# Moving the cast of the normalised rows from ScalarE to VectorE in a post-norm transformer layer

## Chip, cores and metric

One Trainium2 chip, all 8 cores, each working on one sequence of the batch with no exchange between them. The metric is the device time in microseconds of the slowest core. Five engines of a core appear below: TensorE (PE; its weight loads are PEld), VectorE (DVE), ScalarE (ACT), GpSimd (POOL) and SyncE (SP).

## What is computed

One layer on x of shape (8, 4096, 1024), f32: attention inside blocks of 64 tokens with 16 heads of 64, output projection, residual and LayerNorm; then a gated feed-forward part with hidden size 3072, residual and LayerNorm.

```python
qkv = x @ W_qkv.T + b_qkv
attn = softmax(q*scaling @ k.T) within each block of 64 tokens
x = layernorm(x + (attn @ v) @ W_out.T + b_out)
h = silu(x @ (w_gate/127).T) * (x @ (w_up/127).T)
x = layernorm(x + h @ (w_down/127).T)
```

## The kernel before

A core works on its 4096 tokens in 16 tiles of 256, each tile in two blocks `st` of 128 tokens. `tile_front(t)` does V, attention, output projection and the first LayerNorm for one tile; `front_a(t)` does what comes ahead of it: cast of x to bf16 (L355), eight transposes per block through TensorE (L364), their copy out of PSUM (L371), and the 128 QK products of 256 columns (L389), which ScalarE evacuates (L397). Two tiles make a pair `s`, and `ffn(s)` does the feed-forward part for both: gate and up (L783), down (L838), second LayerNorm. The order, written out by hand, is for each pair: `tile_front(2s)`, `front_a(2s+1)`, `tile_front(2s+1)`, `front_a(2s+2)`, `ffn(s)`. In the first pair a stage is added that transposes the feed-forward weights by DMA (SyncE's queue, L289; stores by GpSimd's).

Every engine runs its own instructions strictly in this order; between engines there are semaphores. `P.do(engine, ...)` records one instruction; `inc` names the semaphore that it raises, `waits` what it waits for. A wait on the own engine's semaphore is left out unless it has a `!`. `P.acq` and `P.rel` hand over PSUM buffers: `ps23` is held by one user at a time.

The place of the change is the end of `tile_front`. The output projection of block 1 (L579, L585) ends; VectorE adds the residual (L591) and sums (L640), ScalarE squares (L651), small steps give mean and variance (L658 to L677), and VectorE normalises both blocks, L684, in place in `x1` (f32). Then for each block: a copy of its 1024 columns to bf16 in `aoT` (L698), eight transposes through TensorE into `ps23` (L706), and a copy out of PSUM into `x1T` by VectorE (L714), which releases `ps23` for the next block. In VectorE's order `front_a` of the next tile follows; after the last tile `ffn` does. `emit_qkv_chunk` in the setup has a cast of the same form on VectorE (L225).

Of the kernel before, what the change touches and what calls it, by code (L numbers as in the profile page):

```python
# [11 lines left out]
AF = mybir.ActivationFunctionType  # L12
# [87 lines left out]
def build_nc(n_tiles=NT, dbg=False):  # L100
# [5 lines left out]
    wout = nc.dram_tensor("wout", [E, E], F32, kind="ExternalInput").ap()  # L106
# [33 lines left out]
    with ExitStack() as ctx:  # L140
# [13 lines left out]
        aoT = en(nc.sbuf_tensor("aoT", [128, 2048], BF16))  # L154
# [29 lines left out]
        def body(P: Prog):  # L184
            mil = {}

            def xsrc(t):
                return x_in[t * TTOK:(t + 1) * TTOK, :].rearrange("(st pp) j -> pp st j", pp=128)
# [5 lines left out]
            for t in range(min(2, n_tiles)):  # L194
                P.do("gpsimd", lambda s, t=t: s.dma_start(
                    out=xf[:, (t % 2) * 2048:(t % 2) * 2048 + 2048].rearrange("p (st j) -> p st j", st=2),
                    in_=xsrc(t)), inc="sx" + str(t % 2), amt=16)
                mil["xload", t] = P.c["sx" + str(t % 2)]
            P.do("scalar", lambda s: s.activation(out=brow[0:1, 0:E], in_=stgb[0:1, :], func=AF.Copy),
                 inc="sc", waits=[("sp1", mil["consts"])])  # L200
            mil["bcast1"] = P.c["sc"]
            P.do("gpsimd", lambda s: s.dma_start(out=stgb[:], in_=bv_in), inc="sp4", amt=16,
                 waits=[("sc", mil["bcast1"])])
            mil["bvload"] = P.c["sp4"]
            P.do("scalar", lambda s: s.activation(out=brow[0:1, E:2 * E], in_=stgb[0:1, :], func=AF.Copy),
                 inc="sc", waits=[("sp4", mil["bvload"])])
            mil["bcast"] = P.c["sc"]
            P.do("vector", lambda v: v.tensor_scalar_mul(bqkvT[:, 0:KCH], bqkvT[:, 0:KCH], QSCALE),
                 inc="ve", waits=[("sp1", mil["consts"])])
# [3 lines left out]
            for cc in range(2):  # L213
                P.do("gpsimd", lambda g, cc=cc: g.dma_start(
                    out=wout_nat[:, cc * 512:(cc + 1) * 512],
                    in_=wout[:, cc * 512:(cc + 1) * 512]), inc="sgo" + str(cc), amt=16)
# [45 lines left out]
            for k in range(KCH):  # L262
                P.do("sync", lambda s, k=k: s.dma_start(  # L263
                    out=RWout[:, k * E:(k + 1) * E],
                    in_=wout_nat[:, k * 128:(k + 1) * 128], transpose=True),
                    inc="sp3", amt=16, waits=[("sgo" + str(k // 4), 16)])
# [143 lines left out]
            def tile_front(t):  # L410
# [8 lines left out]
                for st in range(2):  # L419
                    w = P.acq("ps23") + [("sc", mil["bcast"]), ("ve", mil["xt_evac", t, 1])]  # L420
                    for half in range(2):
                        for k in range(KCH):
# [5 lines left out]
                                waits=w if (half == 0 and k == 0) else ())  # L428
# [4 lines left out]
                            inc="pe" if half == 1 else None)  # L433
                    mil["v_mm", t, st] = P.c["pe"]
                    P.do("vector", lambda v, st=st: v.tensor_copy(  # L435
                        out=vtok[:, st * 1024:(st + 1) * 1024], in_=ps23[:]),
                        inc="ve", waits=[("pe", mil["v_mm", t, st]),
                                         ("sb2", mil.get("dump_vtok", 0))])
# [3 lines left out]
                if dbg and t == DBG_T:  # L442
                    P.do("gpsimd", lambda q: q.dma_start(out=dbg_t["d_xT"], in_=xT[:]),
                         inc="sb0", amt=16, waits=[("ve", mil["xt_evac", DBG_T, 1])])
                    mil["dump_xT"] = 16
                    P.do("gpsimd", lambda q: q.dma_start(out=dbg_t["d_qkT"], in_=qkT[:]),
                         inc="sb1", amt=16, waits=[("sc", mil["qk_done", DBG_T])])
                    mil["dump_qkT"] = 16
                    P.do("gpsimd", lambda q: q.dma_start(out=dbg_t["d_vtok"], in_=vtok[:]),
                         inc="sb2", amt=16, waits=[("ve", mil["v_evac", DBG_T, 1])])  # L450
# [166 lines left out]
                if t + 2 < n_tiles:  # L617
                    P.do("gpsimd", lambda s, t=t: s.dma_start(
                        out=xf[:, (t % 2) * 2048:(t % 2) * 2048 + 2048].rearrange("p (st j) -> p st j", st=2),
                        in_=xsrc(t + 2)), inc="sx" + str(t % 2), amt=16,  # L620
                        waits=[("ve", mil["resid1", t, 1])])
# [7 lines left out]
                if dbg and t == DBG_T:  # L629
                    P.do("gpsimd", lambda q: q.dma_start(out=dbg_t["d_aoT"], in_=aoT[:]),  # L630
                         inc="sb5", amt=16, waits=[("ve", mil["aoT", DBG_T, 1, 1])])
                    mil["dump_aoT"] = 16
                    P.do("gpsimd", lambda q: q.dma_start(out=dbg_t["d_x1a"], in_=x1[:, (DBG_T % 2) * 2048:(DBG_T % 2) * 2048 + 2048]),
                         inc="sb6", amt=16, waits=[("ve", mil["resid1", DBG_T, 1])])
                    mil["dump_x1a"] = 16

                if STAGE <= 7:
# [6 lines left out]
                    inc="ve", waits=[("ve!", mil["resid1", t, 1])])  # L644
                mil["lnsum", t] = P.c["ve"]
                for st in range(2):
                    pssq = ps45 if st == 0 else ps67
                    psname = "ps45" if st == 0 else "ps67"
                    xsl = x1[:, x1off + st * 1024: x1off + (st + 1) * 1024]
                    w = P.acq(psname)  # L650
                    P.do("scalar", lambda sC, xsl=xsl, pssq=pssq, st=st: sC.activation(  # L651
                        out=pssq[:], in_=xsl, func=AF.Square,
                        accum_out=stats[:, Q1 + st:Q1 + st + 1]),
                        inc="sc",
                        waits=w + [("ve", mil["resid1", t, st])])
# [4 lines left out]
                    inc="ve", waits=[("ve!", mil["lnsum", t])])  # L660
# [4 lines left out]
                    inc="ve", waits=[("ve!", mil["mean1", t])])  # L665
# [4 lines left out]
                    inc="ve", waits=[("sc", mil["square", t, 1]), ("ve!", mil["msq1", t])])  # L670
                mil["var1", t] = P.c["ve"]
                P.do("scalar", lambda sC: sC.activation(
                    out=stats[:, R1:R1 + 2], in_=stats[:, V1:V1 + 2], func=AF.Ln,
                    bias=stats[:, EPSC:EPSC + 1]),
                    inc="sc", waits=[("ve", mil["var1", t])])
                mil["lnln1", t] = P.c["sc"]
                P.do("scalar", lambda sC: sC.activation(  # L677
                    out=stats[:, R1:R1 + 2], in_=stats[:, R1:R1 + 2],
                    func=AF.Exp, scale=-0.5),
                    inc="sc", waits=[("sc!", mil["lnln1", t])])  # L680
                mil["rstd1", t] = P.c["sc"]
                for st in range(2):
                    xsl = x1[:, x1off + st * 1024: x1off + (st + 1) * 1024]
# [3 lines left out]
                        inc="ve", waits=([("sc", mil["rstd1", t]),  # L687
                                          ("sb6", mil.get("dump_x1a", 0))] if st == 0 else ()))
                    mil["norm1", t, st] = P.c["ve"]

                if dbg and t == DBG_T:
                    P.do("gpsimd", lambda q: q.dma_start(out=dbg_t["d_x1"], in_=x1[:, (DBG_T % 2) * 2048:(DBG_T % 2) * 2048 + 2048]),
                         inc="sb7", amt=16, waits=[("ve", mil["norm1", DBG_T, 1])])
                    mil["dump_x1"] = P.c["sb7"]

                for st in range(2):
                    xsl = x1[:, x1off + st * 1024: x1off + (st + 1) * 1024]
                    P.do("scalar", lambda sC, xsl=xsl, st=st: sC.activation(  # L698
                        out=aoT[:, st * 1024:(st + 1) * 1024], in_=xsl, func=AF.Copy),
                        inc="sc",  # L700
                        waits=[("ve", mil["norm1", t, st]), ("pe", mil["wout", t, 1]),
                               ("sb5", mil.get("dump_aoT", 0))])
                    mil["x1b", t, st] = P.c["sc"]
                    w = P.acq("ps23")
                    for c in range(KCH):
                        P.do("tensor", lambda tn, st=st, c=c: tn.matmul(  # L706
                            ps23[:, c * 128:(c + 1) * 128],
                            aoT[:, st * 1024 + c * 128: st * 1024 + (c + 1) * 128],
                            ident[:], start=True, stop=True),
                            inc="pe" if c == KCH - 1 else None,  # L710
                            waits=(w + [("sc", mil["x1b", t, st])]) if c == 0 else ())
                    mil["x1t_mm", t, st] = P.c["pe"]
                    l = p * 2 + st
                    P.do("vector", lambda v, l=l: v.tensor_copy(  # L714
                        out=x1T[:].rearrange("p (k j) -> p k j", j=512)[:, :, l * 128:l * 128 + 128],
                        in_=ps23[:].rearrange("p (k j) -> p k j", j=128)),
                        inc="ve",
                        waits=[("pe", mil["x1t_mm", t, st]),
                               ("pe", mil.get(("gu_done", s - 1), 0) if (t % 2 == 0 and st == 0) else 0)])
                    mil["x1t_evac", t, st] = P.c["ve"]  # L720
                    P.rel("ps23", "ve")
# [207 lines left out]
            for s in range(n_tiles // 2):  # L929
                tile_front(2 * s)  # L930
                if STAGE <= 8:
                    break
                if not EARLY_A:
                    front_a(2 * s + 1)
                if s == 0:
                    emit_prep_casts2()
                tile_front(2 * s + 1)
                if not EARLY_A and 2 * s + 2 < n_tiles:
                    front_a(2 * s + 2)
                ffn(s)  # L940
                if STAGE <= 10:
                    break
# [76 lines left out]
```

How the kernel before makes its waits and increments, by code:

```python
    def do(self, engname, emit=None, inc=None, amt=1, waits=()):  # L67
        if engname == self.live:
            eng = self.eng[engname]
            for (s, v) in waits:
                force = s.endswith("!")
                if force:
                    s = s[:-1]
                if v <= 0 or (SEM_PROD[s] == engname and not force):
                    continue
                if v <= self._waited[s]:
                    continue
                eng.wait_ge(self.sems[s], v)
                self._waited[s] = v
            inst = emit(eng)
            if inc is not None:
                inst.then_inc(self.sems[inc], amt)
        if inc is not None:
            self.c[inc] += amt
# [99 lines left out]
        def body(P: Prog):  # L184
# [751 lines left out]
                    emit_prep_casts2()  # L936
                tile_front(2 * s + 1)
                if not EARLY_A and 2 * s + 2 < n_tiles:
                    front_a(2 * s + 2)
                ffn(s)
                if STAGE <= 10:
                    break
            for nm in SEM_PROD:
                if P.c[nm] > 0 and SEM_PROD[nm] != "sync":
                    P.do("sync", lambda sq, nm=nm, v=P.c[nm]: sq.wait_ge(sems[nm], v))
            for nm in SEM_PROD:
                if P.c[nm] > 0 and SEM_PROD[nm] == "sync":
                    P.do("sync", lambda sq, nm=nm, v=P.c[nm]: sq.wait_ge(sems[nm], v))
```

## Time and profile before

| | us |
|---|---|
| runs of the kernel | 2730.4, 2891.5 (median 2811.0) |
| profiled execution, its own time | 2741.3 |
| its span on the slowest core | 2739.8 |
| TensorE products busy | 2022.0 (74% of the span) |
| VectorE busy | 799.3 (29%) |
| ScalarE busy | 469.0 (17%) |

The span runs from the first to the last instruction of the slowest core. Busy time tells how much an engine did, not whether something waited for it; that is in the chain of work that ended last, and in the idle time before an instruction together with what ended it. "PEclk" is the clock that TensorE was granted, as a share of 2.4 GHz.

### The profile page before, as it was taken

To read this page: it belongs to the slowest core of one execution; us is meant where nothing else is said; L and a number is where in the kernel's file an instruction comes from. 1 tells how busy PE (TensorE), PEld (TensorE's weight loads), DVE (VectorE), ACT (ScalarE), POOL (GpSimd) and SP (SyncE) were. 2 spreads that over 40 slices of the span, in tenths; PEclk is the share of its full clock that TensorE was granted. 3 is DMA by queue.
4 is the path that set the end of the run, shared out by engine and by line. 5 is a ranking of instruction groups with operands and counts; after the bars stand their busy time and mean duration, and the time that the engine had idled before them with its cause. 6 is when DMAs were issued, how large, how long until landed. Compare 5 with 4: busy or idle time off the path is not lost.

```text
span 2739.8 us, 27267 instructions; the slowest of 8 cores (2720.8 to 2739.8 us)
## 1 busy us (share of the span) xinstructions
PE 2022.0 (74%) x10560; PEld 999.3 (36%) x10560; DVE 799.3 (29%) x1282; ACT 469.0 (17%) x867; POOL 66.9 (2%) x111
## 2 busy tenths in 40 slices
PE   1567229776797679976797678976698588976795
PEld 1333214224443335434443344434443244433342
DVE  2443001043321441143322432143311532133411
ACT  0112101012210122012211122112211122112210
POOL 1100000100000000000000000000000000000000
PEclk9967669867898679977799678977799678987798
DMA  9999994620143002510053102510043102520033
GB/s 168 164 113 124 222 230 148 134 97 31 39 142 128 16 32 79 159 54 31 16 154 108 47 30 71 159 64 31 16 139 123 46 16 77 154 77 16 23 116 108
DMA packets 258830, 253.55 MB, mean 93 GB/s; under 512 B 88608, under 2 KB 221744, under 8 KB 258128
## 3 DMA queue, kind: packets, MB, share of 16 engines
q1 hardware_dynamic: 216576, 121.65, 17.7%
q0 software_dynamic: 19280, 86.11, 14.2%
q10 hardware_dynamic: 22848, 44.05, 4.9%
q8 instruction: 87, 1.43, 0.2%
q14 instruction: 39, 0.32, 0.0%
HBM read 216.13 MB, written 56.62 MB: 100 GB/s over the span
## 4 chain that ended last, share of the span: by engine, by line
PE 57%; DVE 15%; SPq 9%; DMA 9%; issue 3%; another core or an unknown queue 3%; ACT 3%; DVEq 0%; POOL 0%; ACTq 0%; POOLq 0%
PE ps L783 24%; PE ps L389 8%; PE ps L838 8%; SPq L289 7%; PE ps L579 6%; DMA wdb<-wdT_s 4%; PE ps L423 3%; DMA wdb<-wd_nat 2%; DVE diag L508 2%; DVE stats L491 2%; PE ps L472 2%; PE ps L466 2%; SPq L263 2%; DVE x L861 1%
## 5 line engine op out<-in xcount | busy, mean ns | idle before, releaser
L783 PE MATMUL ps<-x1T,wgu 128*128 128x512 bf16 x3072 | 670.9, 381 | 98.6 <-DMA wgu<-wuT_s 97.1
L783 PEld LDWEIGHTS ps<-x1T,wgu 128*128 128x128 bf16 x3072 | 301.9, 98 | 465.0 <-issue 108.4
L838 PE MATMUL ps<-wdb,hT 128*128 128x512 bf16 x1536 | 351.3, 385 | 51.9 <-DMA wdb<-wdT_s 23.3
L801 DVE TENSOR_TENSOR hT<-silu,ps 128x512 bf16<-128x512 bf16 x192 | 132.0, 688 | 751.1 <-PE ps L783 519.9
L389 PE MATMUL ps<-xT,RWqkv 128*128 128x256 bf16 x2048 | 260.5, 295 | 23.6 <-DVE xT L371 23.6
L838 PEld LDWEIGHTS ps<-wdb,hT 128*128 128x128 bf16 x1536 | 146.8, 99 | 256.4 <-issue 97.8
L389 PEld LDWEIGHTS ps<-xT,RWqkv 128*128 128x128 bf16 x2048 | 201.6, 105 | 82.3 <-issue 27.4
L423 PE MATMUL ps<-RWqkv,xT 128*128 128x512 bf16 x512 | 146.0, 437 | 87.0 <-DVE vtok L435 60.0
L579 PE MATMUL ps<-RWout,aoT 128*128 128x512 bf16 x512 | 179.1, 513 | 35.1 <-DVE aoT L567 35.1
L795 ACT ACTIVATE silu<-ps 128x512 bf16<-128x512 f32 x192 | 114.6, 597 | 523.5 <-PE ps L783 523.4
L397 ACT ACTIVATE qkT<-ps,bqkvT_s 128x256 bf16<-128x256 f32 x256 | 121.4, 474 | 401.1 <-PE ps L389 401.1
L861 DVE SCALAR_TENSOR_TENSOR x<-ps,x 128x1024 f32<-128x1024 f32 x32 | 37.0, 1218 | 397.6 <-PE ps L838 397.6
L706 PE MATMUL ps<-ident_s,aoT 128*128 128x128 bf16 x256 | 32.3, 305 | 145.6 <-ACT aoT L698 120.0
L466 PE MATMUL ps<-qkT 64*128 64x128 bf16 x512 | 136.1, 266 | 0.0
L472 PE MATMUL ps<-augcS 4*128 4x128 bf16 x512 | 136.0, 266 | 0.0
L479 ACT ACTIVATE expb<-ps 128x1024 bf16<-128x1024 f32 x64 | 65.5, 1024 | 339.8 <-PE ps L472 339.8
L435 DVE CAST vtok<-ps 128x1024 bf16<-128x1024 f32 x32 | 39.2, 1224 | 282.0 <-PE ps L429 282.0
L423 PEld LDWEIGHTS ps<-RWqkv,xT 128*128 128x128 bf16 x512 | 50.8, 107 | 164.2 <-issue 129.8
L491 DVE TENSOR_REDUCE stats<-expb 128x8 f32<-128x1024 bf16 x64 | 78.0, 1220 | 98.7 <-ACT expb L479 95.8
L870 ACT ACTIVATE ps<-x 128x1024 f32<-128x1024 f32 x32 | 32.9, 1028 | 422.4 <-DVE x L861 422.4
L579 PEld LDWEIGHTS ps<-RWout,aoT 128*128 128x128 bf16 x512 | 56.8, 121 | 131.2 <-issue 112.1
L508 DVE TENSOR_SCALAR diag<-ident_s,stats 128x128 bf16<-128x128 bf16 x512 | 89.3, 251 | 45.3 <-ACT stats L501 45.3
(71 smaller groups left out, 1080.2 us busy)
## 6 DMA issues: line engine op xcount, KB each, us to landing
wgu<-wgT_s SPq DMA_DIRECT2D x64, 768.0 KB, 4.9
wgu<-wuT_s SPq DMA_DIRECT2D x64, 768.0 KB, 6.9
wdb<-wdT_s ACTq DMA_DIRECT2D x84, 512.0 KB, 3.6
xf<-x POOLq DMA_DIRECT2D x16, 1024.0 KB, 5.2
y<-x POOLq DMA_DIRECT2D x16, 1024.0 KB, 5.6
x<-wqkv POOLq DMA_DIRECT2D x24, 512.0 KB, 10.9
wg_nat<-wg POOLq DMA_DIRECT2D x1, 6144.0 KB, 64.1
wu_nat<-wu POOLq DMA_DIRECT2D x1, 6144.0 KB, 122.4
```

The lines of the kernel that those rows point to most:

```text
L289: P.do("sync", lambda q, nat=nat, k=k, stg=stg: q.dma_start(out=stg, in_=nat[:, k * 128:(k + 1) * 128], transpose=True), inc="spt" + str(p ...
L389: P.do("tensor", lambda tn, c=c, k=k, bank=bank: tn.matmul(ps01[:, bank * 512:bank * 512 + 256], RWqkv[:, k * 3 * E + c * 128: k * 3 * E + ...
L397: P.do("scalar", lambda sC, c=c, bank=bank: sC.activation(out=qkT[:, c * 256:(c + 1) * 256], in_=ps01[:, bank * 512:bank * 512 + 256], fun ...
L423: P.do("tensor", lambda tn, st=st, half=half, k=k: tn.matmul(ps23[:, half * 512:(half + 1) * 512], xT[:, k * 256 + st * 128: k * 256 + st ...
L466: P.do("tensor", lambda tn, st=st, slot=slot, qpo=qpo, qc=qc, kc=kc, pst=pst: tn.matmul(pst[:, slot * 128:(slot + 1) * 128], qkT[qpo:qpo + ...
L472: P.do("tensor", lambda tn, slot=slot, qpo=qpo, pst=pst: tn.matmul(pst[:, slot * 128:(slot + 1) * 128], augcS[qpo:qpo + 4, 0:128], augcS[q ...
L491: P.do("vector", lambda v, col=col, eo=eo: v.reduce_sum(stats[:, SUMS + col * 8:SUMS + col * 8 + 8].rearrange("p (g o) -> p g o", g=8), ex ...
L508: P.do("vector", lambda v, h8=h8, hh=hh, eo=eo: v.tensor_scalar_mul(diag[:, eo + h8 * 128:eo + (h8 + 1) * 128], ident[:], stats[:, RCPC + ...
L579: P.do("tensor", lambda tn, st=st, half=half, k=k: tn.matmul(ps23[:, half * 512:(half + 1) * 512], aoT[:, k * 256 + st * 128: k * 256 + st ...
L783: P.do("tensor", lambda tn, wi=wi, k=k, mi_=mi_, boff=boff, pair=pair: tn.matmul(pair[:, wi * 512:(wi + 1) * 512], wgu[:, boff + wi * (KCH ...
L801: P.do("vector", lambda v, m=m, pair=pair: v.tensor_tensor(hT[:, m * 512:(m + 1) * 512], silu2[:, (m % 2) * 512:(m % 2 + 1) * 512], pair[: ...
L838: P.do("tensor", lambda tn, m=m, l=l, half=half, wslot=wslot, coff=coff: tn.matmul(psl[l][:, half * 512:(half + 1) * 512], hT[:, m * 512 + ...
```

## The change

The two f32 to bf16 copies of each tile at L698 are issued to VectorE as `tensor_copy` instead of to ScalarE as an activation with `Copy`. Their semaphore is VectorE's, TensorE waits for that one, and each copy waits explicitly for the normalisation of its block, which is on the same engine. In VectorE's order a tile now reads: both L684, copy of block 0, L714 of block 0, copy of block 1, L714 of block 1. Nothing else is changed: 32 instructions in all.

```diff
-                    P.do("scalar", lambda sC, xsl=xsl, st=st: sC.activation(
-                        out=aoT[:, st * 1024:(st + 1) * 1024], in_=xsl, func=AF.Copy),
-                        inc="sc",
-                        waits=[("ve", mil["norm1", t, st]), ("pe", mil["wout", t, 1]),
+                    P.do("vector", lambda v, xsl=xsl, st=st: v.tensor_copy(
+                        out=aoT[:, st * 1024:(st + 1) * 1024], in_=xsl),
+                        inc="ve",
+                        waits=[("ve!", mil["norm1", t, st]), ("pe", mil["wout", t, 1]),
                                ("sb5", mil.get("dump_aoT", 0))])
-                    mil["x1b", t, st] = P.c["sc"]
+                    mil["x1b", t, st] = P.c["ve"]
                     w = P.acq("ps23")
                     for c in range(KCH):
                         P.do("tensor", lambda tn, st=st, c=c: tn.matmul(
@@
-                            waits=(w + [("sc", mil["x1b", t, st])]) if c == 0 else ())
+                            waits=(w + [("ve", mil["x1b", t, st])]) if c == 0 else ())
```

## Rows read from the trace of the kernel before

**Rows 1.** Spans and mean granted TensorE clock of the cores.

```profile
core 5: 2739.8 us, clock 0.828
...
core 7: 2720.8 us, clock 0.832
```

**Rows 2.** The chain that ended last, by engine, from the page.

```profile
PE 57%; DVE 15%; SPq 9%; DMA 9%; issue 3%; another core or an unknown queue 3%; ACT 3%; DVEq 0%; POOL 0%; ACTq 0%; POOLq 0%
```

**Rows 3.** Groups by line: busy us, mean ns; idle before, what ended it.

```profile
L783 PE MATMUL ps<-x1T,wgu 128*128 128x512 bf16 x3072 | 670.9, 381 | 98.6 <-DMA wgu<-wuT_s 97.1 <-DVE x1T L714 1.5
L838 PE MATMUL ps<-wdb,hT 128*128 128x512 bf16 x1536 | 351.3, 385 | 51.9 <-DMA wdb<-wdT_s 23.3 <-DMA wdb<-wd_nat 20.0 <-DVE hT L801 7.5
...
L397 ACT ACTIVATE qkT<-ps,bqkvT_s 128x256 bf16<-128x256 f32 x256 | 121.4, 474 | 401.1 <-PE ps L389 401.1
...
L706 PE MATMUL ps<-ident_s,aoT 128*128 128x128 bf16 x256 | 32.3, 305 | 145.6 <-ACT aoT L698 120.0 <-DVE x1T L714 25.6
...
L698 ACT ACTIVATE aoT<-x 128x1024 bf16<-128x1024 f32 x32 | 32.0, 1049 | 17.1 <-DVE x L684 17.1
...
L684 DVE TENSOR_SCALAR x<-x,stats 128x1024 f32<-128x1024 f32 x32 | 24.6, 810 | 12.7 <-ACT stats L677 12.7
```

**Rows 4.** Timeline of tile 7's end: start, us, instructions, idle before.

```profile
1332.24 1.53 DVE L684 TENSOR_SCALAR x<-x,stats 128x1024 f32<-128x1024 f32 x2 [0.79 <-ACT stats L677]
1333.20 2.00 ACT L698 ACTIVATE aoT<-x 128x1024 bf16<-128x1024 f32 x2 [1.07 <-DVE x L684]
...
1334.40 1.01 PE L706 MATMUL ps<-ident_s,aoT 128*128 128x128 bf16 x8 [7.48 <-ACT aoT L698]
1335.52 1.23 DVE L714 CAST x1T<-ps 128x1024 bf16<-128x1024 f32 x1 [1.75 <-PE ps L706]
...
1336.99 1.01 PE L706 MATMUL ps<-ident_s,aoT 128*128 128x128 bf16 x8 [1.58 <-DVE x1T L714]
1338.11 1.23 DVE L714 CAST x1T<-ps 128x1024 bf16<-128x1024 f32 x1 [1.37 <-PE ps L706]
1339.25 1.22 DVE L355 CAST xb<-xf 128x2048 bf16<-128x2048 f32 x1
...
1340.62 1.01 PE L364 MATMUL ps<-ident_s,xb 128*128 128x128 bf16 x8 [2.61 <-DVE xb L355]
```

**Rows 5.** Line L225: duration in ns min/median/max, first and last start.

```profile
L225 DVE CAST hT<-x x24: 682/693/741, 41.7 to 105.9; 128x1024 bf16<-128x1024 f32 x24
```

**Rows 6.** The chain in order of time, first stage: start, us, what.

```profile
163.49 116.10 SPq L289
```

**Rows 7.** Timeline of ScalarE, tiles 1 and 0.

```profile
271.71 2.00 ACT L698 ACTIVATE aoT<-x 128x1024 bf16<-128x1024 f32 x2 [1.07 <-DVE x L684]
...
187.03 2.00 ACT L698 ACTIVATE aoT<-x 128x1024 bf16<-128x1024 f32 x2 [1.07 <-DVE x L684]
```

**Rows 8.** The chain, QK stretches of tiles 6 and 7, and of tile 8.

```profile
1260.62 17.02 PE ps L389 x128
...
1345.59 15.54 PE ps L389 x128
...
1571.42 16.93 PE ps L389 x128
```

**Rows 9.** Stretches of 1 us: busy time of engines, PEclk, DMA share, GB/s.

```profile
1266.00:1267.00 1.00, 1.00 (x9) 0.76 (x8) 0.00 (x0) 0.46 (x1) 0.00 (x0) 0.73 0.00 0
...
1348.00:1349.00 1.00, 1.00 (x9) 0.79 (x8) 0.00 (x0) 0.05 (x2) 0.00 (x0) 0.77 0.00 0
```

**Rows 10.** The chain, gate and up products of pairs 6 and 7.

```profile
2292.98 82.89 PE ps L783 x384
...
2581.99 85.76 PE ps L783 x384
```

**Rows 11.** The chain, first V products of tiles 6 and 8 on it.

```profile
1195.84 3.57 PE ps L423 x8
...
1508.26 3.57 PE ps L423 x8
```

## The prediction

> **What bounds the kernel now.** First the cores: the spans lie between 2720.8 (core 7) and 2739.8 us (core 5), at a mean clock near 0.83, so core 5 stands for the chip [rows 1]. Then the chain that ended last, by line: TensorE's products carry 57% of it and VectorE 15%; ScalarE has only 3% [rows 2]. So the engine that loses work here (ScalarE) is not a bound, and the one that gains it (VectorE) sits on the chain. What matters is the place of the moved copy, and for that the groups by line: all 16 first copies of a tile are waited for by TensorE, 120.0 us of idle time for L706 (7.5 each, the whole LayerNorm among them), and a further 25.6 us go to the wait for the VectorE copy out of PSUM at L714 [rows 3]. In every tile the transposes of x1 are thus a relay in which TensorE has nothing else to do.
>
> **The relay before, in one tile.** The timeline of tile 7 shows it [rows 4]. Normalisations (L684) start at 1332.24 and run 1.53 us for two; ScalarE's copies start at 1333.20 (2.00 for two); transposes at 1334.40; L714 at 1335.52; second transposes at 1336.99; second L714 at 1338.11; the next tile's cast L355 at 1339.25; its transposes at 1340.62. From first normalisation to first transposes: 2.16 us. From the first L714 to the second transposes: 1.47, which is L714 alone, because the second ScalarE copy ended at 1335.20, long before.
>
> **The change, part by part.** It takes 32 copies off ScalarE (1.05 us each [rows 3]) and gives VectorE 32 copies from an f32 tile in SBUF to a bf16 tile in SBUF, 128x1024. The trace has exactly this form on VectorE at L225: 0.682 to 0.741 us, median 0.693 [rows 5]. Bounds: below, half of the 128x2048 cast L355, 0.61; above, the same size out of PSUM, L714, 1.23 [rows 4]. I take 0.69. It is 0.36 shorter than ScalarE's, but order counts more, as VectorE works its program in order: both normalisations, copy 0, L714 of block 0 (which waits for TensorE), copy 1, L714 of block 1.
>
> First transposes: the second normalisation now stands before copy 0. A normalisation takes 0.81 [rows 3] and the two 1.53, so they start 0.72 apart and copy 0 starts 1.44 to 1.53 after the first; then 0.69, and 0.15 from VectorE's end to TensorE's start (L355 at 1339.25 plus 1.22, transposes at 1340.62 [rows 4]). That is 2.28 to 2.37 against 2.16: 0.12 to 0.21 later. I take 0.12, since satisfied waits still let VectorE's instructions follow closely (L355 started 0.09 before L714 had ended [rows 4]).
>
> Second transposes: copy 1 now stands behind the first L714. It starts 1.14 after L714 does (as L355 behind the second L714, 1339.25 - 1338.11), then 0.69 + 0.15: 1.98 against 1.47, 0.51 later. This copy lay free beside the transposes and now lies on the path. What follows (second L714, L355, its transposes) keeps its distances. Sum: 0.12 + 0.51 = 0.63 us later per tile.
>
> The new waits are on VectorE's own normalisations, which have ended when they are reached: nothing. TensorE's wait changes its semaphore, not its number: nothing. Behind the removed copies on ScalarE stands only the evacuation of the next QK products, for which it sat idle 401.1 us [rows 3], so an earlier free ScalarE brings nothing. Behind the added copies on VectorE stand L714, L355 and, for odd tiles, the first product of the feed-forward part (it waited 1.5 us for L714 in the last pair [rows 3]). No DMA is moved; the load of x on GpSimd waits for L591, ahead of all this.
>
> How often it counts: tiles 0 and 1 (ScalarE's copies at 187 and 272 us) lie inside the first stage, where the chain is in the weight transposes on the SyncE queue, from 163.49 us for 116.10 in one piece, to 279.6 [rows 6, 7]. Their 0.63 is hidden by that. Tiles 2 to 15 count: 14 x 0.63 = 8.8 us if nothing else moved.
>
> **The clock.** What follows the relay is a stretch of 128 QK products (L389), begun at the low level (0.50, 1.2 GHz) and finished at the full one (1.00, 2.4 GHz). After an even tile it took 16.9 to 17.0 us in all seven cases, after an odd one 15.5 in all six [rows 8]. The difference is the moment at which the clock rises: tile 6's stretch starts at 1260.62 and the clock rises at about 1266.54, 5.9 us on (0.73 in that microsecond); tile 7's starts at 1345.59 and it rises at about 1348.46, 2.9 us on [rows 9]. Setting 5.9 low + 11.1 full and 2.9 low + 12.6 full both equal to 128 products gives 4.7 and 9.0 products per us: a low microsecond does 0.52 of a full one. So if a start comes d later and the rise stays, the end is only 0.52 d later.
>
> Even tile: the start is 0.63 later, the rise 5.3 us on; I take the rise as unmoved, the end is 0.33 later. Odd tile: its start is 0.33 + 0.63 = 0.96 later. With an unmoved rise only 1.9 us of work would stand before it; the rows show 2.9 and 5.9 and nothing shorter. I take it that the rise then comes later, near what even tiles have, and the stretch takes about 16.8 instead of 15.5 (17.0 is the upper end, 15.1 the lower, with the rise unmoved). So 0.96 + 1.3 = 2.26 us per pair for the six pairs from tiles 2 and 3 to 12 and 13: 13.6. The last pair has no QK stretch behind it; its feed-forward part begins low (85.76 against 82.89 us for the same 384 products [rows 10]) and with its rise unmoved gives half of 0.96: 0.5. Sum 14.1 us.
>
> A rule speaks to this: the Trainium skill, "TensorE: Matmul & The Clock Gate", section "Part 1: The HAM clock gate", says that the gate's observation is free-running and that a clock change depends on where the first matmul lands in it. By that rule too a late start can meet the rise late or unmoved; the two kinds of stretch in rows 8 and 9 agree, and the sum above comes from those rows.
>
> After that a pair's delay passes the feed-forward part (VectorE and transfers started by TensorE itself, so they move along) and enters the V products and attention of the next even tile. From V product to QK start this took 64.8 us (1195.84 to 1260.62) in one pair and 63.2 (1508.26 to 1571.42) in another [rows 8, 11], again by where the clock rises. I take 0 on average, with bounds of about 6 us either way (seven pairs, up to 0.8 each).
>
> **The sum.** The profiled execution is 2741.3 us long by its own time (span 2739.8). 2741.3 + 14.1 = 2755. The two runs shown are 2730.4 and 2891.5 with a median of 2811.0; my sum is against the profiled execution and lies near the lower run.
>
> **Rivals.**
> - *The rise stays put after odd tiles too.* The stretch shortens to 15.1 and a pair is 0.96 x 0.52 = 0.5 late: 7 x 0.5 = 3.5, time 2745. For it: the clock does not know of the kernel. Against: no rise under 2.9 us on. 0.15.
> - *Hidden altogether* (the transfers of the down stage, L838, had been late for other reasons and absorb it): 2741. For it: TensorE waited 23.3 us for wdb [rows 3]. Against: those transfers start on TensorE's progress. 0.08.
> - *Faster by the clock in the attention stretch.* With the rise unmoved (3.5) and all seven V-to-QK stretches at their short end (-6): -2.5, time 2739. 0.07.
> - *Faster by the shorter copy.* If the engine's duration alone counted, 14 x 0.36 = 5.0 us would be gained: 2736. For it: 1.05 against 0.69 [rows 3, 5]; against: the order worked out above. The Trainium skill, "Perfetto Trace Analysis", section "Optimizing Scalar/DVE Operations", says an operation that either engine can do is faster on VectorE where a performance mode exists; the durations agree, the order is what it leaves out. 0.05.
> - *The copy runs at the speed of L714*, 1.23: 2 x 0.54 x 14 = 15.1 more, time 2770. For it: all other 1024-wide casts on this path. Against: L225. 0.08.
> - *Slower by over 2%*: the clock stays low for whole QK stretches. 128 products at 4.7 per us are 27.2 us, 10.2 and 11.7 over today's, 22 per pair; from the third pair on it exceeds 55 us, e.g. 2741 + 66 = 2807. Against: it rose in all thirteen. 0.02.
>
> **How the numbers follow.** My forecast has 0.55. The range must hold also the rivals from 2736 to 2770 and the lower run as a base (2730 + 3.5): 2732 to 2775. That leaves out the last rival and the tails of the others, less than 0.2. About 2% (55 us) is what a measurement of this kernel can tell from no change; only the last rival and an error of fourfold reach it: slower 0.03, faster 0.01, same 0.96.
>
> **What would show it.** VectorE copies near 0.69 us with TensorE's second transposes 1.98 after the first L714 began; from first normalisation to the QK start 0.63 longer (13.35 to 13.98); even stretches 16.7, odd ones 16.8. Odd stretches at 15.1 speak for the first rival; copies of 1.2 for the fifth. If VectorE waited before copy 0, or if the spans of both kernels were equal with these distances changed, my account of what lies on the path would be wrong.

## The result and the profile after

| | before | after |
|---|---|---|
| median of all runs, us | 2742.0 (15 runs) | 2813.7 (16 runs) |
| lowest, us | 2729.3 | 2749.2 |
| profiled execution, us | 2741.3 | 2750.3 |
| its spans, eight cores, us | 2720.8 to 2739.8 | 2729.1 to 2748.7 |
| mean of these spans, us | 2728.8 | 2741.5 |

The medians hold runs in which the cores of one die (in one run of both) ran at a lower granted clock, about 0.74 to 0.81, and took up to 200 us longer, 9 of the 16 runs after and 5 of the 15 before, and every ratio below compares only runs without that. By these the changed kernel takes 1.0058 times the time of the kernel before, 95% interval 1.0037 to 1.0079: 16 us more. That is within the 2% called "same" here, but it is a loss.

The timeline of the changed kernel's slowest core, end of tile 7 (start, us, engine, line, instructions, idle time before and what ended it):

```profile
1331.54 1.53 DVE L684 TENSOR_SCALAR x<-x,stats 128x1024 f32<-128x1024 f32 x2 [0.79 <-ACT stats L677]
1332.98 0.69 DVE L698 CAST aoT<-x 128x1024 bf16<-128x1024 f32 x1
...
1333.82 1.01 PE L706 MATMUL ps<-ident_s,aoT 128*128 128x128 bf16 x8 [7.60 <-DVE aoT L698]
1334.94 1.23 DVE L714 CAST x1T<-ps 128x1024 bf16<-128x1024 f32 x1 [1.27 <-PE ps L706]
1336.08 0.69 DVE L698 CAST aoT<-x 128x1024 bf16<-128x1024 f32 x1
...
1336.91 1.01 PE L706 MATMUL ps<-ident_s,aoT 128*128 128x128 bf16 x8 [2.08 <-DVE aoT L698]
1338.03 1.23 DVE L714 CAST x1T<-ps 128x1024 bf16<-128x1024 f32 x1 [1.27 <-PE ps L706]
1339.17 1.22 DVE L355 CAST xb<-xf 128x2048 bf16<-128x2048 f32 x1
```

Beside [rows 4]: first transposes 2.28 us after the first normalisation (before 2.16), second transposes 1.97 after the first L714 (before 1.47). The copy itself takes 0.69 instead of 1.05, and VectorE never sits idle ahead of it (0.0 in its row below); but copy 1 starts only at 1336.08, 1.14 after L714 started. The groups by line say the same in one row: TensorE's idle time ahead of L706 grew from 145.6 to 155.2 us and all of it now ends on the copy (in [rows 3] 25.6 us ended on L714):

```profile
L706 PE MATMUL ps<-ident_s,aoT 128*128 128x128 bf16 x256 | 32.4, 307 | 155.2 <-DVE aoT L698 155.2
...
L698 DVE CAST aoT<-x 128x1024 bf16<-128x1024 f32 x32 | 21.9, 686 | 0.0
```

The QK stretches in the chain of work in order of time (start, us, what), an even tile and the odd one after it, and the microsecond in which the clock rises in the odd one (columns as in [rows 9]):

```profile
1260.21 16.70 PE ps L389 x128
...
1345.51 16.72 PE ps L389 x128
```

```profile
1349.00:1350.00 1.00, 1.00 (x7) 0.67 (x6) 0.00 (x0) 0.47 (x1) 0.00 (x0) 0.50 0.00 0
1350.00:1351.00 1.00, 1.00 (x7) 0.72 (x6) 0.00 (x0) 0.12 (x1) 0.00 (x0) 0.60 0.00 0
```

In [rows 8] the odd stretch took 15.54. Now the clock rises at 1350.8, 5.3 us after the stretch began, where before it was 2.9, so the odd tile pays 1.2 us more, and the even one 0.3 less because its start comes later while its rise stays.

One slowest core is a thin base, so the following table takes all eight cores of each profiled execution: from the timelines, the time in pieces of the program, added up per core and averaged. "Front" is everything from the end of one down stage to the QK start, from the QK end to the next QK start, and in the last pair to the first feed-forward product: 14 relays, all exposed. "QK" is the 7 even and 6 odd stretches. "Transfer-bound" is the first stage and the down stages, which differ by several us between executions of whatever kernel. The last columns are the mean odd stretch and how many of 48 odd stretches had their clock rise under 4.4 us after their start. Stretches are counted here to the start of their last product, 0.11 us less than in rows that give their length. What the table leaves out, mostly the gate and up products, is 616 to 617 us in each of the three executions.

| us, mean of 8 cores | front | QK | transfer-bound | odd stretch | early rises |
|---|---|---|---|---|---|
| before | 1030.1 | 210.7 | 871.8 | 15.61 | 41 |
| before, a second execution | 1030.6 | 211.0 | 870.2 | 15.65 | 40 |
| after | 1039.5 | 215.2 | 870.7 | 16.59 | 0 |

Front +9.4 and QK +4.5: 13.9 us. These two are the change; the two executions of the kernel before differ in them by 0.5 and 0.3. They are sums over parts of the program, and stand beside the 12.7 us by which the mean span grew and the 16 us (10 to 22) of the ratio.

### The profile page after: what moved, and what is told of

The parts are those of the page before. It is cut to its first block, busy times and chain, and to the rows that moved or that the text cites. A ratio compares the mean times of both kernels' runs of the same rounds, so it can differ in the third digit from the quotient of the medians.

```text
span 2748.7 us, 27253 instructions; the slowest of 8 cores (2729.1 to 2748.7 us)
## 1 busy us (share of the span) xinstructions
PE 2021.3 (74%) x10560; PEld 1002.4 (36%) x10560; DVE 817.8 (30%) x1314; ACT 436.5 (16%) x835; POOL 67.1 (2%) x111
## 3 DMA queue, kind: packets, MB, share of 16 engines
q0 software_dynamic: 19280, 86.11, 14.1%
## 4 chain that ended last, share of the span: by engine, by line
PE 56%; DVE 15%; DMA 9%; SPq 9%; issue 4%; another core or an unknown queue 3%; ACT 2%; DVEq 0%; POOL 0%; ACTq 0%; POOLq 0%
PE ps L783 24%; PE ps L389 8%; SPq L289 8%; PE ps L838 7%; PE ps L579 6%; DMA wdb<-wdT_s 5%; PE ps L423 3%; DMA wdb<-wd_nat 2%; PE ps L472 2%; PE ps L466 2%; DVE diag L508 2%; DVE stats L491 2%; DVE x L861 1%; DVE stats L880 1%
## 5 line engine op out<-in xcount | busy, mean ns | idle before, releaser
L389 PE MATMUL ps<-xT,RWqkv 128*128 128x256 bf16 x2048 | 267.9, 300 | 23.9 <-DVE xT L371 23.6
L389 PEld LDWEIGHTS ps<-xT,RWqkv 128*128 128x128 bf16 x2048 | 205.7, 107 | 85.8 <-issue 28.2
L423 PE MATMUL ps<-RWqkv,xT 128*128 128x512 bf16 x512 | 144.7, 434 | 87.1 <-DVE vtok L435 60.1
L706 PE MATMUL ps<-ident_s,aoT 128*128 128x128 bf16 x256 | 32.4, 307 | 155.2 <-DVE aoT L698 155.2
L423 PEld LDWEIGHTS ps<-RWqkv,xT 128*128 128x128 bf16 x512 | 50.6, 107 | 163.2 <-issue 128.3
```

Source lines behind the costliest of these rows:

```text
L389: P.do("tensor", lambda tn, c=c, k=k, bank=bank: tn.matmul(ps01[:, bank * 512:bank * 512 + 256], RWqkv[:, k * 3 * E + c * 128: k * 3 * E + ...
L423: P.do("tensor", lambda tn, st=st, half=half, k=k: tn.matmul(ps23[:, half * 512:(half + 1) * 512], xT[:, k * 256 + st * 128: k * 256 + st ...
```

## Experiments

Each ratio is to the kernel before, measured beside it on the same chip; front and QK are against the first row of the table. The theory: the order in VectorE's queue lengthens the relay by 0.63 us per tile, and the later start of odd QK stretches costs them the early clock rise.

**Only block 0's copy moved.**

```diff
-  P.do("scalar", ... out=aoT[block st], in_=x1[block st])
+  P.do("vector" if st == 0 else "scalar", ...)
```

> Only block 0's copy is on VectorE, block 1's stays on ScalarE. My theory (place in VectorE's order): first transposes 2.28 us after the first normalisation instead of 2.16, second transposes still 1.47 after the first L714, first normalisation to QK start 13.47 (before 13.35, after 13.97); the QK stretch after odd tiles keeps its early clock rise and stays at 15.4 to 15.5 us; the whole +1 to +2 us over before. Rival A (the copy's own duration counts, 0.69 for 1.05): 5 us faster than before. Rival B (any copy on VectorE costs alike): half of the change's loss, +8.

Measured: 2742.1 and 2743.6 us, too few comparable runs for an interval, so only the trace speaks. First normalisation (1323.99) to QK start (1337.47) 13.48 us, as expected. Front +3.6 over before (expected 1.7), QK +2.5. But only 19 of 48 odd stretches kept the early rise; I had expected all. Core 0 has both kinds, an odd stretch at 709.58 and one at 1644.95:

```profile
709.58 15.45 PE ps L389 x128
...
1644.95 17.06 PE ps L389 x128
```

The early rises that are left came 2.63 to 2.73 us after the start (before: 2.64 to 2.87 in two executions), the others 5.4 to 6.0. The kernel before sat next to the edge: 0.12 us more is enough for many to fall over it. Front and QK together, 6.1 us, lie nearer to rival B's 8 than to my 1 to 2; what speaks against B is the relay, 0.13 us longer here and 0.49 in the next kernel.

**Only block 1's copy moved** (`st == 1` in the line above).

> Only block 1's copy is on VectorE. Theory: first transposes at 2.16, second transposes 1.98 after the first L714, first normalisation to QK start 13.86; stretch after odd tiles goes over to the late clock rise, about 16.8; the whole +11 to +14 us. Rival B (any copy on VectorE costs alike): +8. Rival A: faster.

Measured: 1.0043 (1.0017 to 1.0069), 12 us; normalisation to QK start 1328.06 to 1341.90, 13.84; no early rise left, odd stretches 16.66; front +7.7, QK +3.1. The copy that lay beside the transposes is the one that costs, four times what copy 0 adds to the relay.

**Both copies on VectorE, but ahead of L714.**

```diff
   for st in range(2):
       P.do("vector", ... tensor_copy(out=aoT[block st], in_=x1[block st]))
+  for st in range(2):
       transposes (L706); copy out of PSUM (L714)
```

> Both copies on VectorE as in the changed kernel, but both ahead of block 0's L714 in its order. Theory: copy 1 lies beside the first transposes, second transposes at 1.47 after L714, first normalisation to QK start 13.47; odd stretches 15.4 to 15.5; the whole +1 to +2 us over before. Rival (VectorE's added work or its memory traffic costs, not the order): the same +16 as the changed kernel.

The timeline of tile 7 (L707 and L715 are L706 and L714 there):

```profile
1323.88 1.53 DVE L684 TENSOR_SCALAR x<-x,stats 128x1024 f32<-128x1024 f32 x2 [0.79 <-ACT stats L677]
1325.33 1.29 DVE L698 CAST aoT<-x 128x1024 bf16<-128x1024 f32 x2
...
1326.16 1.01 PE L707 MATMUL ps<-ident_s,aoT 128*128 128x128 bf16 x8 [7.60 <-DVE aoT L698]
1327.28 1.22 DVE L715 CAST x1T<-ps 128x1024 bf16<-128x1024 f32 x1 [0.66 <-PE ps L707]
...
1329.77 1.23 DVE L715 CAST x1T<-ps 128x1024 bf16<-128x1024 f32 x1 [1.26 <-PE ps L707]
```

With the same 32 copies on VectorE the relay is back to 13.37 us (1323.88 to 1337.25, before 13.35): the front is +1.0 instead of +9.4. So the lengthening comes from the order, not from VectorE's added work. It is 0.1 shorter than I had put it, because the two L715 start 2.49 apart where the two L714 of [rows 4] start 2.59 apart. The trace shows why: from the first of them to the second transposes it is 1.37 us in all 128 tiles of the eight cores, before 1.48 in 116 of 128 (1.47 by the rounded times of [rows 4]). Ahead of the second transposes the kernel before has TensorE wait for VectorE's L714 and then for ScalarE's copy, which had ended long ago; with both copies ahead, `P.do` leaves the wait for the copy out, as an earlier wait on the same semaphore covers it. A wait that is already satisfied thus costs 0.1 us where it stands behind the one that ends last. Yet the whole is 1.0038 (1.0004 to 1.0072), 10 us, not the 1 to 2 us expected: 33 of 48 odd stretches rise late, QK is +5.6. That is the clock's part nearly alone. The interval overlaps the changed kernel's, so the whole time doesn't decide between theory and rival here; the front does. Whether the 0.02 us in the relay, or the 0.1 us between the end of an even QK stretch and the start of the odd one (68.07 against 67.97 on the mean), is what tips them was not separated.

**A delay and nothing else.** The kernel before with an idle cast ahead of L355:

```diff
+ P.do("vector", lambda v: v.tensor_copy(out=silu2[:, 0:1024], in_=xf[first 1024 columns]))
  P.do("vector", ... tensor_copy(out=xb[:], in_=xf[...]))      # L355
```

> The kernel before with both copies on ScalarE and an extra VectorE cast of 1024 columns, whose result nothing uses, ahead of every L355, so the QK start comes 0.6 us later without any other part of the change. Theory: even stretches 16.7, odd 16.8 (late rise), the whole +13 to +16 us, like the changed kernel. Rival (the clock's part is not from the delay but from the engines' order or the last pair): odd stretches stay 15.5 or shrink to 15.1 and the whole is +4 to +9 us.

Measured: 1.0045 (1.0028 to 1.0062), 12 us. First normalisation (1331.83) to QK start (1345.79) is 13.96 us, as in the changed kernel. No early rise left, odd stretches 16.60; front +7.3, QK +2.9. It is a little below the expected 13 to 16 and its interval overlaps the changed kernel's. The change's loss comes back, with both copies on ScalarE, from a late QK start alone.

**The delay doubled.** A second such cast (to `expb`).

> As the delay-only kernel, but with two idle casts: the QK starts come 1.2 us later than before instead of 0.6. Theory (the clock's part is a step already taken at the first 0.6 us, further delay only shifts within it): odd and even rises about 4.0 to 4.8 us after the start, stretches 16.2 to 16.4, no longer than in the delay-only kernel; whole +4 to +10 us over the delay-only kernel, i.e. 1.006 to 1.008 times before. Rival (each delay costs in proportion, step or not): twice the delay-only kernel's loss, 1.009.

Measured: 1.0064 (1.0047 to 1.0081), 18 us over before, 5 more than with one cast. Front +14.4, another 7.1; but QK is 1.0 us under the kernel before, 3.9 less than with one cast. The chain of core 5, an even and an odd stretch (L396 is L389 there):

```profile
1878.32 15.47 PE ps L396 x128
1961.96 16.30 PE ps L396 x128
```

Odd rises now come 4.0 to 4.7 us after the start, odd stretches 16.26. The clock's cost is a step, taken at the first tenths of a microsecond; more delay gives part of it back (an odd stretch is 0.65 us longer than before, where one cast made it 0.99). Doubling the delay doubled the front's loss and cancelled the stretches' loss.

**TensorE kept busy through the relay.** Products nobody uses, in idle time, from tile 2 on: 30 ahead of the first x1 transposes, 4 ahead of the second, 9 ahead of the first x transposes, 4 and 4 behind.

```diff
+ def fill(n, ps): n times matmul(ps[:, 0:512], RWqkv[:, 0:128], RWqkv[:, 0:512])
+ fill(30 if st == 0 else 4, ps01)     # ahead of L706, block st
+ fill(9, ps01); fill(4, ps67)         # ahead of L364, blocks 0 and 1
+ fill(4, ps67)                        # ahead of L389
```

> The kernel before, with products that nothing uses put into TensorE's idle time around the transposes of x1 and of the next x (30 ahead of the first x1 transposes, 4, 9, 4 and 4 in the gaps behind, from tile 2 on), so that the QK stretch starts at full clock. Theory (both stretches pay for a low start): QK stretches of 14.2 us after even and odd tiles alike, the fillers lie in idle time: about 7 x 2.7 + 6 x 1.3 = 27 us faster than before. Rival: the fillers themselves delay the relay, or the clock falls all the same, and nothing is gained.

Measured: 0.9841 (0.9828 to 0.9854), 44 us faster, where 27 were expected. Timeline of core 0, tile 7 (L720, L728, L374 and L401 are L706, L714, L364 and L389; L356 is the filler, of whose four products in the second row one has no record):

```profile
1306.21 0.61 PE L720 MATMUL ps<-ident_s,aoT 128*128 128x128 bf16 x8 [0.90 <-ACT aoT L710]
...
1306.87 0.81 PE L356 MATMUL ps<-RWqkv 128*128 128x512 bf16 x3
...
1311.62 0.61 PE L374 MATMUL ps<-ident_s,xb 128*128 128x128 bf16 x8 [0.67 <-DVE xb L361]
...
1315.79 14.15 PE L401 MATMUL ps<-xT,RWqkv 128*128 128x256 bf16 x128 [0.61 <-DVE xT L381]
```

All 104 stretches are at 14.0 to 14.2 us (QK -28.1). What I had left out are the four groups of transposes, 0.61 us instead of 1.01, each on the relay: 1304.05 to 1315.79 is 11.74 us, 1.61 less than before; front -21.0. The first stage, where there are no fillers, took 9.9 us longer in this execution. It did so in all five kernels with fillers of this document: 544.8 to 550.0 us on the mean of the cores, against 537.0 to 541.0 in the nine executions without. Nothing here tells why.

**The same fillers in the changed kernel.**

> The same fillers in the changed kernel. Theory: with the clock's part removed only the longer relay is left, 14 x 0.63 = 9 us over the filled kernel before, QK stretches 14.2. Rival (the change costs as much whatever the clock does): +15 over the filled kernel before.

Measured: 0.9841 (0.9828 to 0.9854), the same as without the change. In the timelines the relay is 12.35 us against 11.74 (1310.63 to 1322.98), and the front is 7.2 us and QK 0.6 longer, 7.8 in all, near the 8.5 that 14 times 0.61 makes. In the whole time this does not show, though the two intervals leave room for only some 5 us either way: the forecast of 9 was missed. In the profiled executions transfer-bound stages were 9.4 us shorter; by the mean span of the eight cores over the four comparable runs of each, the changed kernel is 3.3 us longer (2689.3 against 2686.0, and runs of one kernel differ by more than that). So the direct part is shown in the stages and not in the whole; whether transfers took it up or the runs are too few is open. What is gone is the step in the odd stretches, 14.04 and 14.05.

**No copy on the path.** VectorE writes the normalised block as bf16 at once, and the f32 normalisation in place comes after the next tile's L371.

```diff
- tensor_scalar(x1[st], x1[st], mean, rstd); tensor_copy(aoT[st], x1[st])
+ tensor_scalar(aoT[st], x1[st], mean, rstd)        # bf16, L684
+ tensor_scalar(x1[st], x1[st], mean, rstd)         # f32, after front_a, L695
```

> No copy on the path at all: VectorE writes the normalised block as bf16 into aoT directly (tensor_scalar), and the f32 normalisation in place follows after the next tile's x transposes, beside the QK products. Theory: first transposes 0.95 us after the start of the first normalisation instead of 2.16, relay 1.2 us shorter than before; the QK starts move to where even rises come under 4 us on, even stretches about 15.7, and the whole is 20 to 30 us faster than before. If the clock gave nothing back: 14 x 1.2 = 17 us faster. Rival (the relay is not what sets the end): no change.

Measured: 0.9917 (0.9902 to 0.9932), 23 us faster. Timeline of core 4 (L710 and L718 are L706 and L714):

```profile
1318.78 1.54 DVE L684 TENSOR_SCALAR aoT<-x,stats 128x1024 bf16<-128x1024 f32 x2 [0.79 <-ACT stats L677]
...
1319.74 1.01 PE L710 MATMUL ps<-ident_s,aoT 128*128 128x128 bf16 x8 [6.28 <-DVE aoT L684]
1320.86 1.23 DVE L718 CAST x1T<-ps 128x1024 bf16<-128x1024 f32 x1 [0.54 <-PE ps L710]
...
1322.23 1.01 PE L710 MATMUL ps<-ident_s,aoT 128*128 128x128 bf16 x8 [1.48 <-DVE x1T L718]
...
1330.60 1.53 DVE L695 TENSOR_SCALAR x<-x,stats 128x1024 f32<-128x1024 f32 x2
...
1330.83 15.94 PE L389 MATMUL ps<-xT,RWqkv 128*128 128x256 bf16 x128 [1.48 <-DVE xT L371]
```

The transposes start 0.96 us after the normalisation and the f32 one lies beside the QK products. The relay is 12.05 us, 1.3 shorter: the 1.2 expected, and the 0.1 of the wait that is left out here too. Front -20.0, QK -3.4: as expected even rises mostly moved under 4 us (45 of 56), odd ones to 3.3 to 3.9; even stretches are 16.05 on the mean, not the 15.7 expected.

**Both, with 30 and with 24 fillers.**

> Both: direct bf16 and fillers. Theory: QK stretches 14.2 and relay 1.2 shorter: about 17 us faster than the filled kernel before. Rival: the fillers ahead of the first transposes now reach into the path (30 of them take 6.5 us or more, and the idle time has shrunk to 6.3), so it is no faster than the direct version alone.

> The direct bf16 version with fillers, 24 instead of 30 ahead of the first transposes, so that they end before the transposes' input is there. Theory: 0.2 to 0.4 us per tile from tile 2 on, 3 to 5 us faster than the version with 30, i.e. 0.974 to 0.976 times before; QK stretches still 14.1. Rival (24 are too few to hold the clock): stretches back at 15.5 or more and slower than the version with 30.

Measured: 0.9763 (0.9748 to 0.9777) and 0.9747 (0.9727 to 0.9767); QK 183.2 in both. Direct bf16 takes another 21 us off the filled kernel, where 17 were expected. With 24 instead of 30 fillers the front is only 0.7 us shorter; the expected 3 to 5 us is not shown, the intervals overlap.

**Fillers in the V products too**, 28 between the two blocks of every even tile, where TensorE waits for the second LayerNorm.

> As the former, and 28 fillers more between the V products of the two blocks of every even tile from tile 2 on, where TensorE waits 6.8 us for the second LayerNorm on VectorE. Theory: the second block's first 8 V products take 1.9 instead of 3.6 us and the first scores run at full clock: 2 to 4 us per pair, 14 to 25 us in all, 0.966 to 0.970 times before. Rival (the clock falls again in the attention whatever came before it, and VectorE sets the pace there): at most the 1.7 us of the V products, of which nothing shows, 0.974.

Measured: 0.9704 (0.9685 to 0.9723), 81 us faster than before and the best version of this study. The first products after the wait, in the chain, changed kernel and this one (L437 is L423 there):

```profile
1507.01 3.57 PE ps L423 x8
```

```profile
1467.20 1.89 PE ps L437 x8
```

The way from the down stage to the QK start became 2.0 us shorter per pair (front -14.4 for all), 1.7 of it in this row. By the ratios this kernel is 12 us faster than the one without these fillers, by the front 14: at or just under the low end of what I expected. The attention behind it gained 0.3 us.

**The kernel before once more**, for the spread of the clock's rises.

> The kernel before itself, once more, to see how much the clock's rises vary from one execution to the next. Theory (they follow from the distances in the program): again about 40 of 48 odd stretches with the early rise, 15.6 us on the mean over all cores. Rival (they vary by execution, and the 7 late ones of the first trace were few by chance): 20 or more of 48 late, and then the late rises of the kernel with both copies ahead of L714 are no effect of its order.

Measured: 40 of 48 early, mean odd stretch 15.65 (first trace 41, 15.61). Core 7's odd stretches, four of its six:

```profile
684.54 15.51 PE ps L389 x128
...
998.53 15.52 PE ps L389 x128
...
1309.21 15.50 PE ps L389 x128
...
1934.11 17.03 PE ps L389 x128
```

The pattern belongs to the program's distances and not to one execution, so the 33 late ones with the copies ahead, of which there is one execution, are taken as an effect of that kernel.

## Why the prediction was right or wrong

- **The relay, 0.12 + 0.51.** Right to 0.01 us at each step: 2.28, 1.97 (1.98 forecast), normalisation to QK start 13.97 (13.98). VectorE's copy was 0.69. Copies ahead of L714 take the relay's loss away at equal work; the delay-only kernel brings it back without the move. One reading was off: the 1.47 us before were not "L714 alone" but 1.37, and 0.10 for the second wait; in the changed kernel that wait ends last, so the sum isn't touched.
- **14 exposed tiles, 8.8 us.** The front is +9.4. Tiles 0 and 1 are hidden: the first stage is 540.2 us before and 540.5 after.
- **The clock, even tiles.** Forecast 16.7 us; measured 16.61 to 16.96 on the slowest core, -1.4 us for all seven (all cores), forecast -2.1.
- **The clock, odd tiles.** Forecast 16.8; measured 16.59 to 16.77 on the slowest core. For the six, +5.8 us against the 7.8 of the sum (1.3 each): on the mean an odd stretch grew by 0.98, because 7 of 48 had been late already and the late rise comes at 5.0 to 5.4 and not at 5.9. The prediction's "15.5 in all six" was one core's.
- **The V products and attention, 0 on average.** Their part of the front is included in the +9.4, of which the relays make 8.7 (14 times 0.62); nothing of the feared 6 us either way is seen.
- **The sum.** +14.1 forecast, which is a ratio of 1.0050; measured 1.0058 (1.0037 to 1.0079), and +13.9 in front and QK of the traces. The class, within 2%, was right too. Rivals: the rise did not stay put (0 of 48), nothing was hidden, the attention stretch gave nothing, the shorter copy gained nothing, the copy ran at 0.69, and no stretch stayed low throughout.
- **What was wrong is the base of the predicted time and with it the range.** The step reads "The two runs shown are 2730.4 and 2891.5 with a median of 2811.0; my sum is against the profiled execution and lies near the lower run." It put the median of all runs on the base of one run, 2741.3, and let the range end at 2775. The changed kernel's runs fall in two groups, seven from 2749.2 to 2757.4 us and nine from 2792.6 to 2950.5, and their median, 2813.7, lies in the upper one. The kernel before had ten runs up to 2745.4 and five from 2781.6 to 2928.5, so its median stayed at 2742.0: the base fits the lower group of either kernel, and the forecast time took every run for one of that group. The two runs shown lay 161 us apart, ten times the effect, and that was to be seen: the range should have taken in 2891.5, or the text should have said that only the difference was forecast. The difference of 14 us was not what missed. Whether the change has a part in nine of sixteen against five of fifteen was not tested.
- **What was right by luck.** I did not see how near the early rise was to its edge, and expected 0.12 us more to leave it alone. The experiments with block 0 only and with the copies ahead show an edge just under it. Had the change cost 0.1 instead of 0.63 us per tile, my sum would have said +1 to +2, and the kernel with the copies ahead measured +10 (1 to 20). The sum of 14 is also nearer than its terms: the odd stretches were put 2.0 us too high, and front and even stretches 0.6 and 0.7 too low.

The Trainium skill, "TensorE: Matmul & The Clock Gate", section "Part 1: The HAM clock gate", which the prediction drew on, holds in that the change of level does depend on where the first product lands, as 41, 19 and 0 early rises of 48 for starts 0, 0.12 and 0.63 us later show. For modelling it puts the ramp's cost under 1% of a typical kernel's span. It says so where it speaks of the start of a kernel; here the clock was low at the start of all 104 stretches, and filling TensorE's idle time in 14 relays gave 1.6%.

## What to carry to other kernels

Ask of a moved instruction first what stands around it in the new engine's program order: a copy that is a third faster cost 0.5 us per tile because it went behind an instruction that waits for the very engine it feeds. In a kernel whose TensorE idles in every tile, as here, the clock can turn a small shift into a step: look, in the trace of every core, at how long after the start of a long stretch the clock rises, and whether the shortest of these times lie close together with none below. A change of 0.1 us cost 1.5 us in a stretch there (15.45 to 17.06), and one of 1.2 us gave part of it back. Where TensorE waits only for a relay of other engines, unused products that fit into the waits are worth trying (44 us here), and dropping the copy gained 23 us where moving it lost 16.

## What the runs showed of the hardware

- In the nine profiled executions without fillers (104 stretches over all cores in each) no QK stretch that began at low clock had its rise under 2.61 us after its start. Where the early rises lay near that edge, the late ones came 5.4 to 6.0 us after the start.
- A VectorE instruction whose waits are satisfied starts 0.09 us before the one ahead of it has ended (1336.08 against 1334.94 + 1.23), so the start-to-start time of a 1.23 us copy is 1.14.
- Eight 128-column transposes took 0.61 us with TensorE at full clock and 1.01 at the low one: short work on a relay feels the clock as well.
- A wait of TensorE that is already satisfied cost 0.1 us where it stands behind the one that ends last: from L714's start to the second transposes 1.48 us with two waits, 1.37 with one.
- With the fillers of the relays alone the mean granted clock was 0.87 to 0.88, before 0.83, and the kernel 1.6% faster. Beside this gain the first stage was 4 to 13 us longer in every kernel with fillers than in any without, for a reason not found.
